# A time-mix layer with a routed feed-forward: VectorE results left in PSUM, right-hand sides with time on the partitions, solves in 32x64 tiles

## The chip, the core and the metric

One core of one Trainium2 chip. The time is device time of one launch, in microseconds (us). TensorE, VectorE, ScalarE and GpSimd are called PE, DVE, ACT and POOL in the profile; SP is the queue that issues most DMAs.

## What is computed

The input is x, 8 sequences of 512 steps with 256 channels (16 heads of 16). Cut to what matters:

```python
r, k, v, w, kk, a = projections(x, previous x)      # kk normed per head, b = -kk * a
wt = exp(-exp(w))
def step(s, inp):                                   # s: 16 x 16 for each sequence and head
    q_, w_, k_, v_, a_, b_ = inp
    sa = einsum('bhij,bhj->bhi', s, a_)
    s = s * w_[:, :, None, :] + sa[..., None] * b_[:, :, None, :] + v_[..., None] * k_[:, :, None, :]
    return s, einsum('bhij,bhj->bhi', s, q_)
y = group_norm(scan(step)) * ln_w + ln_b + bonus    # bonus = (r * k * faaaa).sum(head) * v
x1 = layer_norm(x + (y * g) @ Wo.T)
out = layer_norm(x1 + expert(argmax(x1 @ centroids.T), x1))   # 8 experts, 256 -> 1024 -> 256
```

## The kernel before, in words

The 512 steps are cut in 16 blocks of 32 steps (TB); each block is worked on for all 8 sequences and 16 heads at once. Within a block the recurrence is turned into matrix algebra: scores between all pairs of steps (`scores`, L639), the inverse of a unit triangular 32x32 matrix for each of the 128 pairs of sequence and head (GpSimd, `invert`, L1881), and then with R, the right-hand sides, the product of inverse and R (`solve`, L691), read-out (`read_out`, L721), and the next state (`update`, L707, and `next_state`, L1501). All arithmetic is fp32. After the 16 blocks comes a routing stage and then 39 blocks of 128 tokens through the experts, which the change touches only in where two small PSUM results lie.

Each engine runs a fixed list of calls written out by hand, `body(n)` for n from -2 to 18 (TensorE L779, ScalarE L1208, VectorE L1612, SP L508). Body n holds different stages of several blocks: projections and scores of block n+1, transposes of keys and values of block n, the chain R, solve, read-out and state of block n-1, gate and output projection of block n-2, router of block n-3. Nothing is reordered at run time: an engine that waits holds up all that is behind it in its list. Six PSUM banks are a ring, whose order of users is the list at L364; a user of a bank waits until the steps named in `freed` (L351) have read the one before it. The other two banks (`ry_bank`, RY) hold R and the output Y.

What the change touches, in the order of one body on TensorE:

- `read_state` (L665), called for one half f of the channels at the end of a body and for the other half at the start of the next one. Its first loop has 32 matmuls of a 32x32 state tile with a moving operand of 64 columns, 32 that give R and 32 that give the state's part of Y. Its second loop adds the values' part of R, 32 matmuls of 64x32. R comes out with channels on the partitions and time on the columns.
- `keep_r` (VectorE, L1486) copies R with a mask for odd and even heads into Rm, `turn_r` (TensorE, L687) transposes Rm in 2 times 4 transposes of 128x128, and `keep_rt` (ScalarE, L1144) copies the result to RT, with time on the partitions.
- `solve` (L691): for each half, 32 matmuls of 64x64 tiles. The stationary tile holds the inverses of two heads as a block-diagonal matrix whose zeros are written once. Two tiles of the array are used in turn, chosen by e.
- `keep_x` (ScalarE, L1150) and `keep_x_odd` (VectorE, L1495) copy the result into XV.
- The keys' transposes `turn_keys` for the second half stand after `square(n+1, "r")` and after the second `solve`.

A matmul in fp32 is two records of a weight load and two of a matmul in the trace (two passes), so 32 matmuls are "x64" in a PE row.

The inversion runs on GpSimd for block after block: each block is 30 pairs of a multiply (L1894) and an add (L1897). Around it are DMAs, all issued by SP: `scores_to_pairs` (L455) writes the scores to DRAM with 4 DMAs and reads them with one of 512 KB into Up, one (sequence, head) on each partition; `inverse_to_heads` (L470) writes the inverse with one DMA and reads it with 4.

Many VectorE instructions take a projection from a PSUM bank, write an SBUF tile, and a second VectorE instruction then reads two SBUF tiles. Those that matter here: L1378 (four each block), L1410 (k2), L1452 (bt), L1460 (bm, two), L1467 (ao), L1507 (state), L1514 (w). Others read two SBUF tiles before and after the change: L1359, L1366, L1398, L1415 (k3), L1431 (km, two).

## Time and profile before

| | us |
|---|---|
| three runs | 1090.39, 1099.09, 1100.8 (median 1099.09) |
| profiled execution, span from first to last instruction | 1093.4 |
| TensorE busy in it | 1017.8 (93%) |
| VectorE busy | 792.4 (72%) |
| GpSimd busy | 683.2 (62%) |
| ScalarE busy | 542.2 (50%) |
| mean granted TensorE clock | 0.971 |

Of the profiled execution's own time the profile gives the span alone; it lies between the lowest and the median run, 5.7 us under the median. Busy shares are averages over the stages. The blocks take the stretch from about 70 to 745 us, the experts that from 770 us to the end, where GpSimd is nearly idle. Times in a row are us from the start of the span unless they are marked ns; "x64" counts records; a bracket tells how long the engine was idle before and what ended it.

### The profile page before, as it was taken

The numbers are of one execution on the slowest core, as the hardware profiler recorded it, in microseconds if no ns is written. First come the engines' busy times: TensorE is split into PE (matmuls) and PEld (weight loads), VectorE is DVE, ScalarE is ACT, GpSimd is POOL, SyncE is SP. The second block draws the span as 40 slices with busy tenths as digits, with TensorE's granted clock in tenths as the row PEclk, the third lists the DMA queues.
The fourth block names the chain that finished last, engine by engine and source line by source line (L and its number), as shares of the span: only waits on it lengthen the run. The fifth ranks groups of instructions, "written<-read, shape, count | busy, mean of one in ns | idle before, by whom it ended". The sixth has DMA issues, their size and how long they took to land.

```text
span 1093.4 us, 42536 instructions
## 1 busy us (share of the span) xinstructions
PE 1017.8 (93%) x16804; PEld 836.3 (76%) x16805; DVE 792.4 (72%) x1777; ACT 542.2 (50%) x1113; POOL 683.2 (62%) x1135
## 2 busy tenths in 40 slices
PE   8998999999999999999999999589899999999995
PEld 5676777787777786777777778567798988889894
DVE  4776887887887887888888777147466666666663
ACT  4474676686685785776766757122122222222220
POOL 1088888888988988988988869840223332323321
PEclk9998999999999999999999999689999999999998
DMA  4213224134134133243242241828454454545430
GB/s 104 43 18 79 68 35 109 45 68 108 25 89 106 27 89 87 36 98 82 41 98 61 51 99 23 251 62 288 178 184 155 172 167 164 183 145 181 147 127 4
DMA packets 208624, 112.02 MB, mean 102 GB/s; under 512 B 172364, under 2 KB 191952, under 8 KB 208080
## 3 DMA queue, kind: packets, MB, share of 16 engines
q1 hardware_dynamic: 202080, 100.77, 34.1%
q0 software_dynamic: 3744, 8.40, 2.3%
q8 instruction: 122, 2.00, 0.8%
q10 hardware_dynamic: 2640, 0.54, 0.2%
q14 instruction: 38, 0.31, 0.1%
HBM read 85.42 MB, written 26.08 MB: 102 GB/s over the span
## 4 chain that ended last, share of the span: by engine, by line
PE 68%; POOL 13%; DMA 6%; DVE 5%; issue 4%; ACT 1%; SPq 1%; DVEq 0%; ACTq 0%; POOLq 0%
PE bank L561 16%; PE bank L950 12%; PE bank L963 9%; POOL arena L1897 7%; POOL arena L1894 6%; PE bank L699 5%; PE bank L646 5%; PE bank L654 4%; PE ry L963 4%; PE bank L607 3%; PE ry L676 2%; PE ry L728 2%; DMA arena<-scr_n 2%; PE bank L716 1%; DMA arena<-scr_u 1%
## 5 line engine op out<-in xcount | busy, mean ns | idle before, releaser
L1897 POOL TENSOR_TENSOR arena<-arena 128x30 f32<-128x30 f32 (+14 forms) x480 | 295.6, 616 | 37.6
L1894 POOL TENSOR_TENSOR arena<-arena 128x30 f32<-128x30 f32 (+14 forms) x480 | 287.0, 598 | 36.4
L561 PE MATMUL bank<-arena 128*128 128x256 f32 (+2 forms) x992 | 268.3, 408 | 5.6 <-DVE arena L1400 2.7
L561 PEld LDWEIGHTS bank<-arena 128*128 128x128 f32 x992 | 173.3, 196 | 51.7 <-issue 25.4
L950 PEld LDWEIGHTS bank<-arena 128*128 128x128 f32 x1248 | 146.9, 194 | 5.5 <-issue 2.7
L950 PE MATMUL bank<-arena 128*128 128x128 f32 x1248 | 147.4, 277 | 3.2 <-DVE arena L1803 2.5
L1482 DVE TENSOR_TENSOR arena<-bank,arena 128x512 f32<-128x512 f32 x128 | 79.5, 683 | 29.6 <-PE bank L646 29.5
L1293 ACT ACTIVATE arena<-arena 128x1 f32<-128x1 f32 x39 | 11.5, 294 | 176.9 <-DVE arena L1757 176.9
L1928 POOL COPY arena<-arena 128x1 int32 (+1 forms) x39 | 7.1, 181 | 146.7 <-DVE arena L1821 146.7
L963 PE MATMUL bank<-arena 128*128 x416 | 96.4, 385 | 0.1
L699 PEld LDWEIGHTS bank<-arena 64*64 64x64 f32 x2048 | 68.3, 145 | 28.2 <-issue 22.5
L699 PE MATMUL bank<-arena 64*64 64x32 f32 x2048 | 71.4, 228 | 18.1 <-DMA arena<-scr_u 18.1
L963 PEld LDWEIGHTS bank<-arena 128*128 128x128 f32 x416 | 76.9, 190 | 14.4 <-issue 4.9
L654 PE MATMUL bank<-arena 128*128 128x128 f32 x560 | 80.2, 279 | 1.8 <-issue 0.8
L1922 POOL DMA_INDIRECT arena<-scr_x,arena x39 | 41.1, 1053 | 61.2 <-POOL arena L1920 30.3
L654 PEld LDWEIGHTS bank<-arena 128*128 128x128 f32 x560 | 64.0, 142 | 19.6 <-issue 13.4
L646 PE MATMUL bank<-arena 32*128 32x64 f32 x2048 | 68.8, 275 | 9.4 <-issue 8.2
L646 PEld LDWEIGHTS bank<-arena 32*128 32x128 f32 x2048 | 63.8, 188 | 13.5 <-issue 11.1
L1375 DVE SCALAR_TENSOR_TENSOR arena<-bank,arena 128x256 f32<-128x256 f32 x128 | 55.7, 476 | 19.0 <-PE bank L579 19.0
L1930 POOL DMA_INDIRECT out_dram<-arena x39 | 39.7, 1018 | 34.9 <-DVE arena L1787 20.8
L1803 DVE TENSOR_SCALAR arena<-bank,arena 128x128 f32<-128x128 f32 x156 | 44.0, 345 | 23.1 <-issue 18.0
L1308 ACT ACTIVATE arena<-bank,arena 128x128 f32<-128x128 f32 x156 | 44.7, 368 | 26.6 <-PE bank L950 26.5
(174 smaller groups left out, 1775.2 us busy)
## 6 DMA issues: line engine op xcount, KB each, us to landing
arena<-in_W SPq DMA_DIRECT2D x47, 1024.0 KB, 5.0
scr_n<-arena SPq DMA_DIRECT2D x64, 128.0 KB, 2.8
arena<-scr_n SPq DMA_DIRECT2D x16, 512.0 KB, 3.7
scr_u<-arena SPq DMA_DIRECT2D x16, 512.0 KB, 2.8
arena<-scr_u SPq DMA_DIRECT2D x62, 128.0 KB, 2.9
arena<-in_xTp SPq DMA_DIRECT2D x32, 132.0 KB, 4.0
arena<-in_x SPq DMA_DIRECT2D x64, 64.0 KB, 2.1
scr_x<-arena SPq DMA_DIRECT2D x64, 64.0 KB, 2.5
```

Of the source, the lines that this page charges most:

```text
L561: mm = pe.matmul(ring.tile(m, name)[0:rows, to], lhsT, rhs, start=(i == 0), stop=(i == len(terms) - 1))
L646: mm = pe.matmul(ring.tile(m, f"sc{f}{p}")[:, b * 2 * TB:(b + 1) * 2 * TB], bkm[r, f * B + b, :], aq[m % 2][r, f * B + b].rearrange("p x t ...
L654: mm = pe.transpose(ring.tile(m, name)[:, i * P:(i + 1) * P], src, ident)
L699: mm = pe.matmul(ring.tile(m, f"x{f}")[x, at:at + 32], Ux[m % 2][x, f, p, k].rearrange("p h t -> p (h t)"), RT[f][x, k, 32 * p:32 * p + 32 ...
L950: mm = pe.matmul(hidT_ps[t // 4][:, (t % 4) * P:(t % 4 + 1) * P], W1[s][:, k, t * P:(t + 1) * P], xnT[:, k, :], start=(k == 0), stop=(k == ...
L963: mm = pe.matmul(y_ps[s][:, 0:D], hidT[s][:, t, :], W2f[:, bass.ds(e * (FT * D) + t * D, D)], start=(t == 0), stop=(t == FT - 1))
L1308: relu_act.inc(str(t), A(hidT[s][:, t], hidT_ps[0][:, t * P:(t + 1) * P], ACT.Relu, bias=b1f[:, bass.ds(e * FT + t, 1)]))
L1375: xm_ok.inc(m, f"{g}{h}", STT(out=xm[g][:, h], in0=ring.tile(m, f"lo2_{g}")[:, h * COLS:(h + 1) * COLS], scalar=prm(f"maa{g}", h), in1=dx[ ...
L1482: score.inc(m, name, TT(sc[m % 2][:, f, p].rearrange("p k e x t -> p (k e) (x t)"), ring.tile(m, name)[:, :].rearrange("p (b n) -> p b n", ...
L1803: relu_dve.inc(str(t), nc.vector.tensor_scalar(hidT[s][:, t], hidT_ps[1][:, (t - 4) * P:(t - 3) * P], b1f[:, bass.ds(e * FT + t, 1)], 0.0, ...
L1894: inv_ok.inc(f"m{s}", TT(t, U[:, 0:s, s:s + 1].broadcast_to(shape), U[:, s:s + 1, s + 1:TB].broadcast_to(shape), ALU.mult))
L1897: inv_ok.inc(f"a{s}", TT(U[:, 0:s, s + 1:TB], U[:, 0:s, s + 1:TB], t, ALU.add))
```

## The change

Four edits.

1. VectorE leaves intermediate results in the PSUM bank that they came from: `xm_stage` (L1370), `key_gain` and `gain_keys`, `normed_kk`, `removal`, `decay_kk`, `mask_removal`, `next_state`, `normed`. The second instruction of each pair has then one input in PSUM and one in SBUF. The banks come free later (`freed`), "ao" and "bt" change places.
2. R comes out of `read_state` with time on the partitions: stationary and moving operand are exchanged for R, so the first loop has 64 matmuls with 32 columns each in place of 32 with 64. `keep_r` moves to ScalarE as two plain copies; `turn_r` and `keep_rt` are gone.
3. `solve` works on pairs of head pairs, 32 matmuls each of 32x64 tiles, in four positions of the array in turn, two row groups by two column halves, each row group with a PSUM bank of its own. A product has both heads' inverse times both heads' columns; the half that is not wanted is masked in the copies, `keep_x` (VectorE, six instructions of 64x256 each block) and `keep_x_even` (ScalarE, four of 64x128). The inverse's tile has no zeros and half the size. The scores' read becomes 8 DMAs of 64 KB in place of one of 512 KB.
4. Both `turn_keys` of the second half stand earlier in TensorE's list, their copies on ScalarE too; the first of them now waits in the ring for k2 (bank 5, after "ma").

```diff
-        Ux = [v.rearrange("p (f g k h t) -> p f g k h t", f=HALF, g=PAIRS, k=4, h=2)
-              for v in (Ux_flat[:, 0:2048], Ux_flat[:, 2048:4096])]
+        Ux = [v.rearrange("p (f k e h t) -> p f k e h t", f=HALF, k=4, e=2, h=2)
+              for v in (Ux_flat[:, 0:1024], Ux_flat[:, 1024:2048])]
...
-        Rm_flat = take(NB // 2 * P)
-        Rm = Rm_flat.rearrange("p (g o h t) -> p g o h t", g=NB // 2, o=2, h=2)
-        RT = [take(4 * P).rearrange("p (k n) -> p k n", k=4) for _ in range(HALF)]
+        Rs = take(NB * TB).rearrange("p (e g i) -> p e g i", e=2, g=NB // 2)
...
         ring = Ring(banks, [(0, "bk00@5"), (1, "h@2 k@3"), (0, "bk01@2"), (1, "z@1 a@4 kk@5"), (-3, "logit@2"),
-                            (-2, "g@0"), (1, "ma@5 mk@2"), (-1, "rt0@3 rt1@4"), (-2, "wo@0"), (-1, "x1@1"),
-                            (1, "ss@0 r@4"), (0, "bk11@5"), (1, "v@2"), (-1, "x0@3"), (0, "bk10@0 v0@1 v1@4"),
+                            (-2, "g@0"), (1, "ma@5 mk@2"), (-2, "wo@0"), (-1, "x0@1 x1@3"),
+                            (0, "bk11@5"), (1, "ss@0 r@4"), (0, "bk10@5"), (1, "v@2"), (-1, "x2@1 x3@3"), (0, "v0@5 v1@4"),
...
+        heads_of = lambda m, p: Ux[m % 2][pair_rows(p)].rearrange("r f k e h t -> r (f k e h) t")
...
-                sp.dma_start(Up[m % 2].rearrange("p r c -> p (r c)"),
-                             nd.rearrange("f g k e (h s) t -> (f g k e h) (s t)", h=2)).then_inc(n_in, 16)
+                for f in range(HALF):
+                    for p in range(PAIRS):
+                        sp.dma_start(Up[m % 2][32 * p + 16 * f:32 * p + 16 * f + 16].rearrange("p r c -> p (r c)"),
+                                     nd[f, p].rearrange("k e (h s) t -> (k e h) (s t)", h=2)).then_inc(n_in, 16)
...
+                for p in range(PAIRS if m < last else 2):
+                    sp.dma_start(heads_of(m, p), u_rows[p]).then_inc(u_in, 16)
...
                 for b in range(B):
                     for p in range(PAIRS):
                         r = slice(32 * p, 32 * p + 32)
-                        pe.matmul(RY[b % 2][r, f * 4 + b // 2], S[r, f * B + b, :], aq[buf][r, f * B + b],
+                        pe.matmul(RY[b % 2][r, f * 4 + b // 2, 0], aq[buf][r, f * B + b, 0], S[r, f * B + b, :],
                                   start=(f == 0 and b // 2 == 0), stop=False, skip_group_check=True)
+                        pe.matmul(RY[b % 2][r, f * 4 + b // 2, 1], S[r, f * B + b, :], aq[buf][r, f * B + b, 1],
+                                  start=False, stop=False, skip_group_check=True)
                 for b in range(B):
                     for p in range(PAIRS):
                         r = slice(32 * p, 32 * p + 32)
                         v = v_rows_of(b % 2)
-                        mm = pe.matmul(RY[b % 2][r, f * 4 + b // 2, 0], XV[buf][v, f * B + b, r],
-                                       sc[buf][v, f, p, b // 2, b % 2, 0], start=False, stop=False, skip_group_check=True)
+                        mm = pe.matmul(RY[b % 2][r, f * 4 + b // 2, 0], sc[buf][v, f, p, b // 2, b % 2, 0],
+                                       XV[buf][v, f * B + b, r], start=False, stop=False, skip_group_check=True)
                 if f == HALF - 1:
                     chain_pe.inc(m, "R", mm)
 
-            def turn_r(m, f):
-                chain_dve.wait(pe, m, "rme", "rmo")
-                turn(m, f"rt{f}", [Rm_flat[:, (f * 4 + k) * P:(f * 4 + k + 1) * P] for k in range(4)])
-
-            def solve(m, f):
-                ring.wait_empty(pe, m, f"x{f}")
-                chain_act.wait(pe, m, f"rt{f}")
+            def solve(m, w):
+
+                pairs = (2 * w, 2 * w + 1)
+                for p in pairs:
+                    ring.wait_empty(pe, m, f"x{p}")
+                chain_act.wait(pe, m, "re", "ro")
                 pe.wait_ge(u_in, (m + 1) * 64)
-                for k in range(B // 2):
-                    for p in range(PAIRS):
-                        for e in range(2):
-                            x, at = x_rows_of(e), k * P + 32 * p
-                            mm = pe.matmul(ring.tile(m, f"x{f}")[x, at:at + 32], Ux[m % 2][x, f, p, k].rearrange("p h t -> p (h t)"),
-                                           RT[f][x, k, 32 * p:32 * p + 32], start=True, stop=True)
-                ring.fill(m, f"x{f}", mm)
-
-            def x_kept(m, f):
-                chain_act.wait(pe, m, f"x{f}e")
-                chain_dve.wait(pe, m, f"x{f}o")
+                mm = {}
+                for g in range(NB // 2):
+                    for turn in range(2):
+                        for i, p in enumerate(pairs):
+                            e, r = (turn + i) % 2, pair_rows(p)
+                            mm[p] = pe.matmul(ring.tile(m, f"x{p}")[x_rows_of(e), g * 32:(g + 1) * 32],
+                                              Ux[m % 2][r, g // 4, g % 4, e].rearrange("p h t -> p (h t)"), Rs[r, e, g, :],
+                                              start=True, stop=True)
+                for p in pairs:
+                    ring.fill(m, f"x{p}", mm[p])
+
+            def x_kept(m):
+                chain_act.wait(pe, m, "x2a", "x2b", "x3a", "x3b")
+                chain_dve.wait(pe, m, "x0e", "x0o", "x1e", "x1o", "x2o", "x3o")
...
                     keep_busy(2, idle_ps)
                 if has(n - 1):
-                    solve(n - 1, 1)
+                    solve(n - 1, 0)
+                if has(n) and n < last:
+                    turn_keys(n, 1, 1)
                 if has(n + 1):
                     norms(n + 1)
                 if -1 <= n <= 0:
                 if has(n + 1):
                     square(n + 1, "r", 0, 0)
                 if has(n) and n < last:
-                    turn_keys(n, 1, 1)
+                    turn_keys(n, 1, 0)
                 if has(n + 1):
                     square(n + 1, "v", 2, 3)
                 if n == -1:
                     keep_busy(3, ry_bank[0])
                 if has(n - 1):
-                    solve(n - 1, 0)
-                if has(n) and n < last:
-                    turn_keys(n, 1, 0)
+                    solve(n - 1, 1)
                 if has(n):
                     turn_values(n, 0)
...
+            def keep_r(m):
+                if m:
+                    ring.wait_full(act, m - 1, "x2", "x3")
+                chain_pe.wait(act, m, "R")
+                for e, name in enumerate("eo"):
+                    chain_act.inc(m, f"r{name}", A(Rs[:, e], RY[e][:, :, 0], ACT.Copy))
+
+            def keep_x_even(m, p):
+                ring.wait_full(act, m, f"x{p}")
+                x = x_rows_of(0)
+                for h, name in enumerate("ab"):
+                    i = slice(HS * h, HS * h + HS)
+                    chain_act.inc(m, f"x{p}{name}", A(XV[m % 2][x, 0:NB:2, pair_rows(p)][:, :, i],
+                                                      ring.tile(m, f"x{p}")[x, 0:256].rearrange("p (g i) -> p g i", i=32)[:, :, i],
+                                                      ACT.Copy, scale=own_head[x, h:h + 1]))
...
-                    xm_ok.inc(m, f"{g}{h}", STT(out=xm[g][:, h], in0=ring.tile(m, f"lo2_{g}")[:, h * COLS:(h + 1) * COLS],
-                                                scalar=prm(f"maa{g}", h), in1=dx[:, h], op0=ALU.add, op1=ALU.mult))
+                    part = bank[:, h * COLS:(h + 1) * COLS]
+                    xm_ok.inc(m, f"{g}{h}", STT(out=part, in0=part, scalar=prm(f"maa{g}", h), in1=dx[:, h],
+                                                op0=ALU.add, op1=ALU.mult))
                 xm_ok.wait(dve, m, f"{g}1")
-                xm_ok.inc(m, f"x{g}", TT(tt(xm[g]), tt(xm[g]), x_now, ALU.add))
+                xm_ok.inc(m, f"x{g}", TT(tt(xm[g]), by_step(bank), x_now, ALU.add))
...
-                comb.inc(m, "k2", TT(flat(kt), flat(kt), flat(ma), ALU.mult))
+                comb.inc(m, "k2", TT(flat(kt), flat(kt), ring.tile(m, "ma")[:, :], ALU.mult))
...
-                comb.inc(m, "kkn", STT(out=flat(kk), in0=ring.tile(m, "ss")[:, :], scalar=1e12, in1=flat(kk), op0=ALU.min, op1=ALU.mult))
+                comb.inc(m, "kkn", STT(out=ring.tile(m, "ss")[:, :], in0=ring.tile(m, "ss")[:, :], scalar=1e12, in1=flat(kk), op0=ALU.min, op1=ALU.mult))
...
+                comb.wait(dve, m, "kkn", "ao")
+                bank = ring.tile(m, "ss")[:, :]
+                comb.inc(m, "bt", STT(out=bank, in0=bank, scalar=-1.0, in1=flat(at), op0=ALU.mult, op1=ALU.mult))
...
                 proj.wait(dve, m, "iW0", "iW1")
                 comb.wait(dve, m, "bt")
+                removed = by_step(ring.tile(m, "ss")).rearrange("p (k e) t -> p k e t", e=2)
                 for h in range(2):
-                    comb.inc(m, f"bm{h}", TT(bkm_q[:, :, 1:3, h], pair(at), pair(iW[h]), ALU.mult))
+                    comb.inc(m, f"bm{h}", TT(bkm_q[:, :, 1:3, h], removed, pair(iW[h]), ALU.mult))
...
-                comb.inc(m, "ao", TT(aq[m % 2][:, :, 0], tt(kk), Wt[:, :, 0:TB], ALU.mult))
+                comb.inc(m, "ao", TT(aq[m % 2][:, :, 0], by_step(ring.tile(m, "ss")), Wt[:, :, 0:TB], ALU.mult))
...
+            def keep_x(m, p, e):
+                ring.wait_full(dve, m, f"x{p}")
+                x = x_rows_of(e)
+                chain_dve.inc(m, f"x{p}{'eo'[e]}", TT(XV[m % 2][x, e:NB:2, pair_rows(p)],
+                                                      ring.tile(m, f"x{p}")[x, 0:256].rearrange("p (g i) -> p g i", i=32),
+                                                      same_head[x, None, :].broadcast_to([P // 2, NB // 2, 32]), ALU.mult))
...
                 chain_pe.wait(dve, m, "R")
                 ring.wait_full(dve, m, "su")
-                state_dve.inc(m, "sa", TT(S, ring.tile(m, "su")[:, :].rearrange("p (g i) -> p g i", g=NB), S, ALU.add))
+                su = by_step(ring.tile(m, "su"))
+                state_dve.inc(m, "sa", TT(su, su, S, ALU.add))
                 state_dve.wait(dve, m, "sa")
                 comb.wait(dve, m, "wend")
-                state_dve.inc(m, "s", TT(S, S, Wend[m % 3][:, :, None].broadcast_to([P, NB, 32]), ALU.mult))
+                state_dve.inc(m, "s", TT(S, su, Wend[m % 3][:, :, None].broadcast_to([P, NB, 32]), ALU.mult))
...
                 post_act.wait(dve, m, "rstd", "c0", "c1")
-                post_dve.inc(m, "n", TT(flat(yc), flat(yc), ring.tile(m, "var")[:, :], ALU.mult))
+                bank = ring.tile(m, "var")[:, :]
+                post_dve.inc(m, "n", TT(bank, flat(yc), bank, ALU.mult))
                 post_dve.wait(dve, m, "n")
                 comb.wait(dve, m, "u")
-                post_dve.inc(m, "w", TT(flat(yc), flat(yc), flat(ut[m % 3]), ALU.add))
...
                 if has(n - 2):
                     token_stats(n - 2)
                 if has(n - 1):
-                    keep_x_odd(n - 1, 1)
+                    for p in (0, 1):
+                        keep_x(n - 1, p, 0)
+                        keep_x(n - 1, p, 1)
                 if has(n + 1):
                     key_exponent(n + 1)
                     normed_kk(n + 1)
                     decay_reads(n + 1)
+                    decay_kk(n + 1)
                     removal(n + 1)
-                    decay_kk(n + 1)
                     decay_keys(n + 1)
                     bonus_terms(n + 1)
                 if has(n - 1):
-                    keep_x_odd(n - 1, 0)
+                    keep_x(n - 1, 2, 1)
+                    keep_x(n - 1, 3, 1)
                 if has(n + 1):
```

## Rows read from the trace of the kernel before

**Rows 1.** The page: engines, instruction queue, and DMA issues (size, us to landing).
```profile
PE 1017.8 (93%) x16804; PEld 836.3 (76%) x16805; DVE 792.4 (72%) x1777; ACT 542.2 (50%) x1113; POOL 683.2 (62%) x1135
...
q8 instruction: 122, 2.00, 0.8%
...
arena<-scr_n SPq DMA_DIRECT2D x16, 512.0 KB, 3.7
```

**Rows 2.** Waits of PE from 90 to 700 us: total, times, longest.
```profile
PE bank L699 <- DMA arena<-scr_u: 16.2, 6, 9.7
PE bank L646 <- issue: 8.2, 9, 1.6
```

**Rows 3.** Timeline of PE: the first solve of blocks 0 and 13.
```profile
99.97 2.29 PE L699 MATMUL bank<-arena 64*64 64x32 f32 x51 [2.50 <-DMA arena<-scr_u]
...
656.25 1.96 PE L699 MATMUL bank<-arena 64*64 64x32 f32 x61 [1.17 <-DMA arena<-scr_u]
```

**Rows 4.** Busy by stretch, GpSimd alone: one inversion in mid-run, and the last.
```profile
431.75:473.66 41.91, 37.28 (x61) 1.00 0.34 76
687.97:723.45 35.48, 30.86 (x61) 0.71 0.60 175
```

**Rows 5.** Timelines of POOL and of DVE at 406 us.
```profile
406.64 2.99 POOL L1894 TENSOR_TENSOR arena<-arena 128x240 f32<-128x240 f32 x1
409.70 0.66 POOL L1897 TENSOR_TENSOR arena<-arena 128x240 f32<-128x240 f32 x1
...
406.66 1.27 DVE L1460 TENSOR_TENSOR arena<-arena 128x512 f32<-128x512 f32 x2
407.86 1.28 DVE L1431 TENSOR_TENSOR arena<-arena 128x512 f32<-128x512 f32 x2
```

**Rows 6.** Timeline of PE in one body.
```profile
509.68 1.10 PE L676 MATMUL ry<-arena 32*32 32x64 f32 x64
510.70 0.76 PE L682 MATMUL ry<-arena 64*32 64x32 f32 x64
511.39 0.66 PE L654 MATMUL bank<-arena 128*128 128x128 f32 x4
...
517.99 1.92 PE L561 MATMUL bank<-arena 128*128 128x8 f32 x12
...
520.90 1.09 PE L654 MATMUL bank<-arena 128*128 128x128 f32 x8
521.83 1.89 PE L561 MATMUL bank<-arena 128*128 128x256 f32 x8
523.66 2.06 PE L699 MATMUL bank<-arena 64*64 64x32 f32 x64
...
534.03 0.76 PE L728 MATMUL ry<-arena 128*32 128x32 f32 x64
```

**Rows 7.** Timeline of DVE in the same body.
```profile
519.95 0.87 DVE L1520 SCALAR_TENSOR_TENSOR arena<-arena,bank 128x256 f32<-128x256 f32 x2 [1.66 <-PE bank L561]
...
523.83 0.69 DVE L1530 TENSOR_TENSOR arena<-bank,arena 128x512 f32<-128x512 f32 x1 [0.49 <-PE bank L561]
...
525.99 0.65 DVE L1498 COPY arena<-bank 64x512 f32<-64x512 f32 x1
...
529.95 1.17 DVE L1467 TENSOR_TENSOR arena<-arena 128x512 f32<-128x512 f32 x1
531.05 1.11 DVE L1415 TENSOR_TENSOR arena<-arena 128x512 f32<-128x512 f32 x1
...
532.87 0.67 DVE L1498 COPY arena<-bank 64x512 f32<-64x512 f32 x1
```

**Rows 8.** Busy by stretch: us, busy (records) of PE, PEld, DVE, ACT, POOL, clock.
```profile
447.19:470.49 23.30, 21.61 (x760) 17.21 (x761) 20.45 (x35) 15.55 (x27) 21.09 (x29) 1.00 0.22 50
495.39:510.83 15.44, 14.23 (x501) 11.13 (x506) 12.05 (x21) 8.12 (x16) 13.72 (x23) 1.00 0.28 58
```

**Rows 9.** SP's issues of the scores' writes: count, ns min/median/max of one.
```profile
L462 SPq DMA_DIRECT2D scr_n<-arena x64: 574/648/1695, 40.7 to 679.8; - x64
```

**Rows 10.** Timeline of PE: both solves of the last block.
```profile
730.84 5.92 PE L699 MATMUL bank<-arena 64*64 64x32 f32 x128 [1.94 <-DMA arena<-scr_u]
736.69 2.05 PE L728 MATMUL ry<-arena 128*32 128x32 f32 x128
```

124 lines of the change are left out of this document (51 added, 73 removed).

## Prediction

> **What bounds the kernel now.** I read the page first: TensorE is busy 93% of the span, GpSimd 62% [rows 1], and GpSimd is nearly idle behind the blocks, so within them both are close to full. The share alone doesn't say which one ends last. The timeline of PE says how long a body is: the first solve of block 0 starts at 99.97 us, that of block 13 at 656.25, 13 bodies of 42.8 us [rows 3]. An inversion on GpSimd takes 41.9 us from its first instruction to the last [rows 4], so GpSimd works through block after block with about a microsecond to spare, and TensorE is as full. The waits of PE settle who holds whom: six times PE waited at the solve for the inverse's DMA, 16.2 us in total, of which 9.7 are one wait near the end [rows 2]; the rest, 6.5 us, is 0.5 us a body. The other large group is "issue", time in which PE had no instruction although nothing held it. So PE's own list is the longer loop by a hair, GpSimd's loop touches it, and from block 14 on, where PE has less to do, GpSimd ends last.
>
> Two details decide this case. First, what a crowd of small matmuls costs. In two stretches made mostly of them, PE and PEld together have 1521 records in 23.30 us and 1007 in 15.44 us [rows 8]: 15.3 ns a record in both, whatever the mix. "Issue" waits fall in just these stretches, and the instruction queue moved 2.00 MB in 122 pieces, 16 KB each [rows 1]. 2.00 MB by PE's and PEld's 33,609 records is 60 B a record, so a piece holds some 256 of them (an estimate), and 256 records at 15.3 ns are 3.9 us. I read this as a supply limit: a long crowded stretch can't run faster than a piece each 3.9 us. Second, VectorE. From the fill of the gate's bank (517.99 + 1.92 = 519.91) to the first read-out (534.03) PE takes 14.1 us [rows 6]. VectorE's list in the same stretch starts at 519.95 and ends with a copy at 532.87 + 0.67 = 533.54, with a gap of 0.49 in it [rows 7]. Read-out needs that copy. VectorE is 0.5 us from being the bound of this stretch.
>
> **The change part by part.**
>
> *PSUM results.* A GpSimd instruction of 0.66 us took 2.99 at 406.64, while VectorE ran two bm and two km instructions, all with two SBUF inputs [rows 5]. The last inversion, with VectorE mostly idle, takes 35.48 us, one in mid-run 41.91 [rows 4]: VectorE costs GpSimd 6.4 us a block. By my count 18 VectorE instructions a block read two SBUF tiles and 11 of them stop doing so: 6.4 x 11/18 = 3.9 us; bounds 0 and 6.4. The inversion falls to 38.0 us. What this is worth is only what PE waited for it: -0.5 us a body. VectorE itself gains at ao (1.17 us to the 0.69 that instructions with a PSUM input take) and perhaps at k3 (1.11), which keeps two SBUF inputs [rows 7].
>
> *Transposes of R.* Gone: 8 transposes, 1.09 us busy and 0.93 to the next start (520.90 to 521.83) [rows 6], on PE's list: -0.9. ScalarE's two plain copies stand in a part of its list with slack.
>
> *Solves.* Before, two 64x64 tiles in turn: 64 records in 2.06 us [rows 6]. Now four tile positions in turn. The nearest rows with more positions are the read-outs' and R's 64 records at 0.66 to 0.76 us; with no gain it stays 2.06. I take 1.1 each, so -1.9 a body; bounds -2.7 and 0.
>
> *But these two stand in the stretch in which VectorE is close.* PE's 14.1 us would fall to 11.3. VectorE's 13.1 us of work (13.6 less the gap) lose 0.5 at ao and 0 to 0.4 at k3, and get six masked copies for two: the nearest instruction, two of 128x256 in 0.87 us [rows 7], gives 0.43 each, 2.6 for the 1.3 of before: +1.3. So 13.1 - 0.5 + 1.3 = 13.9, or 13.5 with k3. PE waits there for VectorE, and of the 2.8 us it saves 0.2 to 0.6 is left. I take -0.5. Whether the new tiles overlap hardly matters. The new wait of the keys' transposes for k2 is hidden in this too: k2 ends two VectorE instructions, 1.3 us, behind the output projection, and the solve before it takes 1.1.
>
> *read_state.* It gains 64 matmuls a body: 128 pairs of load and matmul, 256 records, less 16 records for the transposes. It lies right in the crowded stretch, after scores and update. Below: the rate of R's two loops together, 128 pairs from 509.68 to 511.39, 1.71 us, or 13.4 ns a pair [rows 6]: 128 pairs, +1.7 us. At the least it could be nothing, since columns times matmuls stay the same. Above: the rate of rows 8, 256 x 15.3 = 3.9 us. Old stretches were not at the limit all the time, new ones will be nearer to it; I take +2.5. Nothing hides it: the wait for VectorE is in the other half of the body.
>
> The Trainium skill ("Runtime: NRT & Kernel Launch", Instruction fetch mechanics) says that crossing a 16 KiB boundary is "mostly hidden", because dispatch is slower than the fetch. By it nothing is added to the issue cost and the sum would stand at the lower 1.7, some 10 us less over the run; the issue waits in small matmuls speak against it here.
>
> *DMAs.* One read of 512 KB (3.7 us to landing [rows 1]) becomes eight. SP spends 0.65 us on an issue of this kind [rows 9], so the last starts 4.5 us later and lands sooner after its issue: together about +1.8 us, between 0 and +4. GpSimd has 4 us of slack by then, so it costs nothing in mid-run, but counts once before the first inversion and once before the last.
>
> *Sum.* Body: -0.5 - 0.5 + 2.5 = +1.5 us, to 44.3. 13 bodies: +19.5. Start: PE's first wait of 2.50 [rows 3] shrinks with the faster inversion: -2. From the scores of block 14 to those of 15: +1.5. The last DMA: +1.8, the last inversion -0.5. The last solves, 5.92 us [rows 10], run on four tiles: -2.4; but read-out must now wait for all copies instead of the first solve's: +1. Total +18.9 us. The profiled execution's span of 1093.4 becomes 1112.3; the runs' median is 5.7 above the span, which I carry over: 1099.1 + 18.9 = 1118.
>
> **Rivals.** *The extra matmuls are free* (18%). Four tiles stream at once and 64 columns become two times 32, so read_state stays at 1.71 us; the supply limit is my reading of an average. Then a body is -0.5 - 0.5 = -1.0, 13 bodies -13, start, tail and the body between -3: 1083, faster. It decides where read_state adds less than 1 us a body. For it: the columns streamed are the same. Against: rows 8, and 128 records of 64 and 32 columns already run at one rate.
>
> *Only the issue cost, and VectorE frees itself* (20%). +1.7 for read_state, k3 and the masked copies at their best (-0.6): body +0.6, 13 bodies +8, edges +1: 1108, no change that a measurement tells.
>
> *The full supply price* (12%): +3.9, or pairs on the same tile that don't overlap, which come to about the same. Body +2.9, 13 bodies +38, edges as in the forecast: 1137.
>
> *The PSUM edit does not do what it says*: inversions stay at 41.9. With bodies of 44.3 GpSimd still isn't the bound, and the time stays within 2 us of the forecast; it is inside it. The trace would show it.
>
> **How the numbers follow.** Forecast 50%, with a range of its own from 1108 to 1130. About 1% (11 us) is what a measurement of this kernel tells from no change. Faster by more: the first rival, 0.18. Within 1% (1088 to 1110): the second rival and the low end of the forecast, 0.28. Slower: 0.54. The range 1085 to 1138 takes in the second and most of the third rival and leaves about 2 in 10 outside, mostly the first. The edits to GpSimd, transposes and solves all point to less time; that the sum comes out above zero rests on one term, read_state.
>
> The Trainium skill ("TensorEngine Tiling (Array Packing)", Instruction Overhead) states about 60 cycles a matmul, the same for 1 column as for 60. By that, as an estimate, the split doubles the first loop, 1.02 us to 2.04 in each call, +2.0 a body in place of +2.5 and about 1111 in all; no row here shows a 32x32 tile with 32 columns.
>
> **What would show it.** Inversions of about 38 us. No wait of PE for the inverse before block 14. Body of about 44.3 us. L676's successors with 128 records each plus 64 of the second loop in 2.7 us or more. Rather more "issue" in the crowded stretch; rows of 256 records at 3.9 us there. PE waiting for VectorE before the first read-out or in the solves' stretch, 1 to 2 us a body. Wrong: read_state at 1.7 to 2.0 us with bodies under 42.3, or PE without any wait between gate and read-out.

## The result, and the profile after

The changed kernel takes 1175.4 us against 1099.9 for the kernel before: ratio 1.068, with an interval of 1.063 to 1.074. I had said 1118, with a range up to 1138. The sign was right, the size a quarter of what came. In the profiled executions the span grew by 82.1 us, from 1093.4 to 1175.5.

First the page of after, to compare with [rows 1]:

```profile
PE 1029.9 (88%) x18724; PEld 825.1 (70%) x18725; DVE 771.7 (66%) x1809; ACT 534.8 (45%) x1145; POOL 623.2 (53%) x1135
...
q8 instruction: 137, 2.24, 0.8%
...
arena<-scr_n SPq DMA_DIRECT2D x128, 64.0 KB, 2.6
```

The granted clock in fortieths of the span (tenths of 2.4 GHz, 9 is 90% or more), the page of before:

```profile
PEclk9998999999999999999999999689999999999998
```

and of after:

```profile
PEclk9998898999988999989889998857999999999998
```

TensorE's busy time grew by 12 us, the span by 82: the time is idle time and slower time, not work. The mean granted clock is 0.935 where it was 0.971. With levels of 1.2 and 2.4 GHz that is 2 x 0.065 x 1175.5 = 153 us at the low level against 2 x 0.029 x 1093.4 = 63.

The length of a body comes from the first solves of blocks 0 and 13, as in [rows 3] (timeline of PE):

```profile
102.45 1.82 PE L705 MATMUL bank<-arena 32*64 32x32 f32 x60 [1.44 <-ACT arena L1051]
...
722.26 1.85 PE L705 MATMUL bank<-arena 32*64 32x32 f32 x64 [2.50 <-DMA arena<-scr_u]
```

(722.26 - 102.45) / 13 = 47.7 us, where it was 42.8. 13 bodies make 63.5 of the 82 us; 2.5 come before them and 16.1 after.

The waits of PE from 90 to 700 us, against [rows 2] (total, times, longest):

```profile
PE ry L688 <- issue: 23.3, 11, 2.5
PE bank L705 <- DMA arena<-scr_u: 7.8, 4, 2.4
PE ry L736 <- issue: 7.3, 7, 1.4
PE bank L650 <- issue: 6.7, 11, 1.2
PE bank L658 <- DVE arena L1424: 5.5, 8, 0.7
PE ry L680 <- issue: 5.1, 6, 1.5
PE bank L658 <- DVE arena L1434: 4.5, 12, 0.4
```

and the only large wait of GpSimd in the same stretch; in before it was 12.5 us in 6 waits:

```profile
POOL arena L1898 <- DMA arena<-scr_n: 120.5, 13, 14.5
```

The largest group is "issue" in the second loop of `read_state`, L688: nothing that the profile shows holds TensorE there, and it has no instruction. An inversion, busy by stretch as in [rows 4], now takes 37.7 us, and GpSimd then stands still until the next scores are in, 8.0 us here and 9.3 on average (120.5 / 13):

```profile
376.29:413.96 37.67, 33.04 (x61) 0.95 0.32 62
```

One stall in full (timeline of PE, one call of `read_state`, the first and last groups of its first loop, then the second loop):

```profile
463.43 0.27 PE L680 MATMUL ry<-arena 32*32 32x32 f32 x7
...
464.66 0.22 PE L682 MATMUL ry<-arena 32*32 32x32 f32 x3
464.82 0.64 PE L688 MATMUL ry<-arena 64*32 64x32 f32 x50
467.64 0.29 PE L688 MATMUL ry<-arena 64*32 64x32 f32 x14 [2.18 <-issue]
```

The first loop, now 64 matmuls and so 128 records, takes 464.82 - 463.43 = 1.39 us; with 32 matmuls of 64 columns, 64 records, it took 1.02 [rows 6]. Where instructions are at hand, 64 records more cost 0.37 us. Then, 50 records later, none are left for 2.18 us.

The trace also tells what these stalls are. PE's and PEld's records grew by 3,840 and the instruction queue by 15 pieces: 256 records a piece, as the prediction had estimated. Counted in PE's whole list, 39 of the 40 issue waits of over 0.3 us between 90 and 700 us (53.4 of 54.3 us; in before 23 of 24, 20.2 us) end at the same place of a piece: the number of records before them leaves 193 to 195 when divided by 256. Two examples, busy by stretch, each from inside one of these stalls to inside the next (PE and PEld stand first; with PE's five other instructions each stretch holds 512, two pieces):

```profile
457.50:466.50 9.00, 6.87 (x254) 4.71 (x253) 5.18 (x10) 3.14 (x5) 1.41 (x5) 0.81 0.43 100
505.90:513.80 7.90, 5.60 (x254) 4.18 (x253) 5.38 (x12) 4.11 (x5) 0.00 (x0) 1.00 0.29 53
```

By the DMA records of the instruction queue, the transfer of a piece ended at 466.22 and PE went on at 467.64. So it is at 34 of the 35 issue waits of over 0.7 us: PE goes on 1.2 to 1.6 us behind the end of a piece's transfer. The first loop uses up 256 records (128 of matmuls and 128 of loads) in 1.39 us; from 500.06 to 515.85 five pieces started 3.8 to 4.1 us apart, and nowhere from 90 to 700 us were two closer than 3.4. The stalls are waits for instructions to be fetched.

Last, a view that I hadn't taken for the prediction: SP's own timeline. First the kernel before, from the scores' writes of a block to the inverse's reads:

```profile
338.91 1.29 SPq L462 DMA_DIRECT2D scr_n<-arena  x2
342.17 0.34 SPq L467 DMA_DIRECT2D arena<-scr_n  x1
342.56 2.28 SPq L452 DMA_DIRECT2D scr_x<-arena  x4
344.94 1.80 SPq L444 DMA_DIRECT2D arena<-in_x  x4
346.83 0.37 SPq L475 DMA_DIRECT2D scr_u<-arena  x1
349.64 2.53 SPq L486 DMA_DIRECT2D arena<-scr_u  x4
```

Then after:

```profile
357.58 7.17 SPq L467 DMA_DIRECT2D scr_n<-arena  x4
367.99 6.39 SPq L474 DMA_DIRECT2D arena<-scr_n  x8
374.42 1.85 SPq L457 DMA_DIRECT2D scr_x<-arena  x4
376.37 1.81 SPq L449 DMA_DIRECT2D arena<-in_x  x4
378.29 0.37 SPq L482 DMA_DIRECT2D scr_u<-arena  x1
381.04 2.57 SPq L491 DMA_DIRECT2D arena<-scr_u  x4
```

The solves that these reads serve (timeline of PE), in before:

```profile
355.68 2.06 PE L699 MATMUL bank<-arena 64*64 64x32 f32 x64
```

and in after:

```profile
386.14 1.13 PE L705 MATMUL bank<-arena 32*64 32x32 f32 x64 [1.55 <-DMA arena<-scr_u]
```

The write of a block's inverse (scr_u) stands in SP's list behind the read of the next block's scores (scr_n). Before, GpSimd finished the inversion at 345.7 and its write was issued at 346.8. After, GpSimd had finished at 361.8 and the write went out at 378.3. This is one of the longest such waits: 6.2 us of its 16.5 pass before the reads begin, 6.4 in the issues of the eight reads, 3.9 in what follows them. In most bodies of after from 180 us on, the reads begin within about 3 us of the inversion's end and the write follows their first issue by 9.3 to 10.6 us, where in before, from 300 us on, it was 4.7 to 6.6. The eight reads hold up not only the next inversion but the finished one.

### The profile page after: what moved, and what is told of

Its sections match the earlier page's. It is cut to its first block, busy times and chain, and to the rows that moved or that the text cites. A ratio compares the mean times of both kernels' runs of the same rounds, so it can differ in the third digit from the quotient of the medians.

```text
span 1175.5 us, 46538 instructions
## 1 busy us (share of the span) xinstructions
PE 1029.9 (88%) x18724; PEld 825.1 (70%) x18725; DVE 771.7 (66%) x1809; ACT 534.8 (45%) x1145; POOL 623.2 (53%) x1135
## 4 chain that ended last, share of the span: by engine, by line
PE 62%; DVE 13%; issue 9%; DMA 8%; SPq 3%; ACT 3%; POOL 1%; DVEq 0%; ACTq 0%; POOLq 0%
PE bank L565 13%; PE bank L957 11%; PE bank L970 8%; PE bank L650 6%; PE ry L970 4%; PE bank L658 3%; SPq L474 2%; PE bank L611 2%; DMA arena<-scr_u 2%; DMA scr_n<-arena 2%; PE ry L680 2%; PE bank L705 2%; PE ry L736 2%; DVE arena L1505 2%; PE bank L724 2%
## 5 line engine op out<-in xcount | busy, mean ns | idle before, releaser
L565 PE MATMUL bank<-arena 128*128 128x256 f32 (+2 forms) x992 | 284.0, 425 | 10.5 <-DVE arena L1414 5.0
L1908 POOL TENSOR_TENSOR arena<-arena 128x30 f32<-128x30 f32 (+14 forms) x480 | 268.6, 560 | 37.6
L1905 POOL TENSOR_TENSOR arena<-arena 128x30 f32<-128x30 f32 (+14 forms) x480 | 253.6, 528 | 36.4
L565 PEld LDWEIGHTS bank<-arena 128*128 128x128 f32 x992 | 179.8, 204 | 68.9 <-issue 36.6
L957 PE MATMUL bank<-arena 128*128 128x128 f32 x1248 | 147.5, 277 | 3.1 <-DVE arena L1814 2.5
L1898 POOL MEMSET arena<- 128x32 f32 x16 | 2.5, 156 | 194.1 <-DMA arena<-scr_n 194.1
L1498 DVE TENSOR_TENSOR arena<-bank,arena 128x512 f32<-128x512 f32 x128 | 79.6, 684 | 34.6 <-PE bank L650 34.6
L658 PE MATMUL bank<-arena 128*128 128x128 f32 x432 | 75.7, 303 | 14.4 <-DVE arena L1424 6.8
L1389 DVE SCALAR_TENSOR_TENSOR bank<-bank,arena 128x256 f32<-128x256 f32 x128 | 56.1, 484 | 46.5 <-PE bank L583 46.5
L658 PEld LDWEIGHTS bank<-arena 128*128 128x128 f32 x432 | 55.2, 155 | 36.4 <-issue 23.1
L650 PEld LDWEIGHTS bank<-arena 32*128 32x128 f32 x2048 | 65.2, 191 | 14.9 <-issue 12.3
L1420 DVE TENSOR_TENSOR arena<-bank,arena 128x512 f32<-128x512 f32 x16 | 11.1, 692 | 84.7 <-PE bank L611 84.7
L705 PE MATMUL bank<-arena 32*64 32x32 f32 x2048 | 39.9, 229 | 24.4 <-DMA arena<-scr_u 19.1
L705 PEld LDWEIGHTS bank<-arena 32*64 32x64 f32 x2048 | 36.5, 144 | 34.8 <-issue 16.0
L680 PEld LDWEIGHTS ry<-arena 32*32 32x32 f32 x2048 | 43.9, 107 | 23.1 <-issue 22.9
```

Of the source, the lines that this page charges most:

```text
L565: mm = pe.matmul(ring.tile(m, name)[0:rows, to], lhsT, rhs, start=(i == 0), stop=(i == len(terms) - 1))
L650: mm = pe.matmul(ring.tile(m, f"sc{f}{p}")[:, b * 2 * TB:(b + 1) * 2 * TB], bkm[r, f * B + b, :], aq[m % 2][r, f * B + b].rearrange("p x t ...
L658: mm = pe.transpose(ring.tile(m, name)[:, i * P:(i + 1) * P], src, ident)
L680: pe.matmul(RY[b % 2][r, f * 4 + b // 2, 0], aq[buf][r, f * B + b, 0], S[r, f * B + b, :], start=(f == 0 and b // 2 == 0), stop=False, ski ...
L705: mm[p] = pe.matmul(ring.tile(m, f"x{p}")[x_rows_of(e), g * 32:(g + 1) * 32], Ux[m % 2][r, g // 4, g % 4, e].rearrange("p h t -> p (h t)") ...
L957: mm = pe.matmul(hidT_ps[t // 4][:, (t % 4) * P:(t % 4 + 1) * P], W1[s][:, k, t * P:(t + 1) * P], xnT[:, k, :], start=(k == 0), stop=(k == ...
```

## The experiments

Two theories stood at first. A: the 64 added matmuls a body stand in a crowd of small ones, in which instructions come in too slowly. B: the other layout, banks held longer and waits for VectorE cost it. Bodies are measured as above, from block 0 to block 13.

**psum_only**: the kernel before with VectorE's results left in PSUM, and

```diff
-(0, "bk10@0 v0@1 v1@4")
+(0, "bk10@5 v0@1 v1@4")
```

> The kernel before with the first part of the change alone: VectorE's intermediate results stay in PSUM, the banks come free later, the last keys' transpose goes to another bank. Theory A (the loss is in the supply of TensorE's instructions, this part is harmless): inversions of 37 to 38 us, no wait of TensorE for the inverse in mid-run, body 42 to 42.5 us, ratio to before 0.985 to 0.995. Rival B (banks held longer make TensorE wait, part of the 75 us is lost here): ratio over 1.01, with waits of TensorE for VectorE of over 1 us a body.

Measured: 0.992 (0.988 to 0.995). Inversions fell to 36.7 us, even more than I had forecast, the body stayed at 42.8, and no wait for VectorE of any size came in. This part does what it says, and by the medians is worth 9 us. Where they come from isn't shown: the profiled execution was the slowest of its seven, 1092.3 us from first to last instruction against 1093.4 in before. B falls for this part.

**split_r**: the kernel before with the same 64 matmuls more, and nothing else.

```diff
-pe.matmul(RY[b % 2][r, f * 4 + b // 2], S[r, f * B + b, :], aq[buf][r, f * B + b],
+for x in range(2):
+    pe.matmul(RY[b % 2][r, f * 4 + b // 2, x], S[r, f * B + b, :], aq[buf][r, f * B + b, x],
```

> The kernel before, but each of read_state's first-loop matmuls is two of 32 columns in place of one of 64: 64 matmuls a body more, nothing else changed, no other layout, no other wait. Theory A: read_state grows from 3.9 to 6.5 to 7.5 us a body, with issue waits in its second loop, body 45.5 to 46.5 us, ratio 1.035 to 1.05, and the mean clock falls from 0.971 to about 0.95. My forecast's own price (2.5 us a body) would be ratio 1.03. Rival B (the other layout and its waits are what costs): ratio 1.00 to 1.01.

Measured: 1.054 (1.049 to 1.058), body 47.1 us, clock 0.950. Waits of PE, 90 to 700 us (L683 is the second loop, L677 the first):

```profile
PE ry L683 <- issue: 22.9, 11, 3.6
PE ry L677 <- issue: 7.8, 11, 1.6
```

This is after's picture, from this edit alone: 59 us, 3.7 a block, and above the 1.05 that theory A had allowed. Its issue waits end at the same place of a 256-record piece as after's (39 of 40, 49.0 us).

**wide_place**: the same number and shape of small matmuls, but 16 each ahead of the wide matmuls of k, r, v and the gate.

```diff
+for i in range(16):
+    r, at = slice(32 * (i % 4), 32 * (i % 4) + 32), 32 * (i // 4)
+    pe.matmul(ring.tile(m, name)[r, at:at + 32], w_sq[r, 3, 0, 0:32], w_sq[r, 3, 1, 0:32], start=True, stop=True)
```

> The kernel before with 64 more small matmuls a block, 32x32 tiles with 32 columns as those that split_r adds, but ahead of the wide matmuls of k, r, v and the gate, 16 each; their results are overwritten. Theory A (instructions come in at a limited rate, wide matmuls let them catch up): only the issue cost of 0.9 to 1.5 us a body, ratio 1.015 to 1.03, no new issue waits at these places. Rival C (an added small matmul costs some 65 ns wherever it stands, as in split_r): 4 us a body, ratio 1.05.

Measured: 1.023 (1.014 to 1.031), clock 0.967: 25 us, 1.6 a block, give or take 9 us. The same count costs 59 us in the crowd. By the length of a body it is +2.4 us (45.2) against +4.3 (47.1). So the place decides about half of the price. A stands.

**no_y**: after without the state's part of Y. **spread**: after with the second `read_state` behind the projection of k.

```diff
-pe.matmul(RY[b % 2][r, f * 4 + b // 2, 1], S[r, f * B + b, :], aq[buf][r, f * B + b, 1],
```

> The kernel after without the 64 matmuls a body that add the state's part to the output Y (that part of the computation is left out). Theory A: read_state back to about 4 us a body, body 43.5 to 44.5, ratio to the kernel before 1.01 to 1.03 in place of 1.068. Rival B: ratio 1.05 to 1.07.

> The kernel after with the second call of read_state moved behind the keys' first transpose, the hidden layer and the projection of k, so that wide matmuls stand between its two calls; the number of instructions is the same. Theory A (it is the crowd that costs, wide matmuls give the supply time to catch up): 1 to 2 us a body less than after, ratio to before 1.04 to 1.055, issue waits in read_state gone or halved. Rival C (each small matmul costs the same wherever it stands): ratio 1.06 to 1.075.

Measured: no_y 1.040 (1.035 to 1.046), which neither theory had: TensorE now waited for the inverse 15 times from 90 to 740 us, 61.2 us in all. Something else holds the body at 45.4 us once the crowd is smaller. spread 1.087 (1.081 to 1.093): a miss. The issue waits in the second loop fell from 23 to 16 us, but the hidden layer now stood ahead of R and waited for VectorE (L1392, 9.8 us in 12), and the clock fell to 0.927. It moved too much at once to tell on A.

**fillers** and its control **before_fillers**: two useless matmuls of 256 columns between the loops of each `read_state`.

```diff
+ahead, name = (m + 2, "lo2_1") if f == 0 else (m + 1, "bk00")
+if ring.takes(ahead, name):
+    ring.wait_empty(pe, ahead, name)
+    keep_busy(2, ring.tile(ahead, name))
```

> The kernel after with two matmuls of 256 columns (0.43 us each at 2.4 GHz) between the two loops of each read_state, into a bank that is free: 1.7 us a body of work that nobody needs. If the stalls of read_state are a supply limit, the fillers stand in time that is lost anyway, issue in its second loop falls from 25 us to under 10, and the cost is under half of their 1.7 us; if TensorE's idle time there is also what brings the half clock, its time falls from 155 us to under 110 and the ratio to 1.055 or less. If neither holds: ratio 1.085 to 1.095.

> The kernel before with the same two matmuls of 256 columns in each read_state as in fillers. Here the stalls are short (4 us in all), so there is little for the fillers to stand in: 1.2 to 2 us a body, ratio 1.015 to 1.03. That they cost nothing in after (1.0585 against 1.0682) is then the stall and the clock of after. If they cost nothing here either, the fillers say nothing on after's stalls: ratio under 1.01.

Measured: after with fillers 1.059 (1.049 to 1.068), no slower than after (1.063 to 1.074) although more is done; that it is faster isn't shown, since the intervals overlap. Before with them 1.016 (1.012 to 1.020), 17 us slower. In after the issue wait of the second loop fell from 23.3 to 13.3 us, and the mean clock rose from 0.935 to 0.958: 2 x 0.042 x 1163.5 = 98 us at the low level in place of 153. The marks set for A were under 10 us of issue wait, under 110 us at the low level, and 1.055 or less: only the second was reached. That the fillers stand in stall time is shown. That the stalls bring the low clock, which then costs more, fits these numbers; the two were not parted.

**keys_later**: after with both moved transposes, and ScalarE's copies of them, further back.

```diff
-(0, "bk11@5"), (1, "ss@0 r@4"), (0, "bk10@5"), (1, "v@2"),
+(1, "ss@0 r@4"), (0, "bk11@5"), (1, "v@2"), (0, "bk10@5"),
```

> The kernel after with the two moved transposes of the keys further back: one behind the projection of r, one behind that of v, and ScalarE's copies of them moved back too. If the new wait for k2 costs (5.5 us in 8 waits of after, and 4.5 us for k's masked copy), 0.5 to 0.8 us a body comes back: ratio 1.055 to 1.06. If it is hidden in a wait for VectorE that comes anyway, as I forecast, or if the crowd of small matmuls behind it takes it back: 1.065 to 1.07.

Measured: 1.063 (1.055 to 1.072). The waits at L658 for VectorE are gone, and 12.3 us at a projection (L565, for e2) stand in their place. Its interval overlaps after's: no gain is shown.

**no_y_four_reads**: the second bound, first try: the scores' read in 4 DMAs.

```diff
-for f in range(HALF):
-    for p in range(PAIRS):
-        sp.dma_start(Up[m % 2][32 * p + 16 * f:32 * p + 16 * f + 16].rearrange("p r c -> p (r c)"),
-                     nd[f, p].rearrange("k e (h s) t -> (k e h) (s t)", h=2)).then_inc(n_in, 16)
+for p in range(PAIRS):
+    sp.dma_start(Up[m % 2][pair_rows(p)].rearrange("p r c -> p (r c)"),
+                 nd[:, p].rearrange("f k e (h s) t -> f (k e h) (s t)", h=2)).then_inc(n_in, 16)
```

> no_y (the kernel after without the state's part of the output) with the scores' read in 4 DMAs of 128 KB in place of 8 of 64 KB. Theory D (in no_y the bound is the round through SP's list: the inverse's write stands behind the issues of the scores' read, so each of them costs 0.65 us a body): 4 issues less are 2.6 us, TensorE's wait for the inverse falls from 61 us to 20 to 35, ratio from 1.040 to 1.00 to 1.02. Rival: the transfers themselves set the round; ratio 1.035 to 1.045.

Measured: 1.111 (1.102 to 1.121), far slower, body 51.5 us. SP's timeline:

```profile
340.02 2.60 SPq L473 DMA_DIRECT2D arena<-scr_n  x4
...
347.49 0.37 SPq L481 DMA_DIRECT2D scr_u<-arena  x1
356.24 2.23 SPq L490 DMA_DIRECT2D arena<-scr_u  x4
```

and, from the view of the DMAs, GB/s in fortieths of the 12 us from 341 to 353:

```profile
GB/s 0 14 0 0 27 55 55 55 51 246 137 167 188 89 65 65 109 205 79 184 184 150 140 147 321 423 396 423 355 41 55 41 55 55 55 55 55 55 48 34
```

The busy share of the 16 DMA engines, in tenths, in the same slices:

```profile
DMA  0200011119456221372665549999811111111110
```

The issues are shorter as planned (2.6 us for the 4.3 to 6.4 of eight), but the reads flow at some 55 GB/s at either end of the stretch, and the inverse's write of 512 KB waits behind them: 8.7 us to landing, where it took 2.7. These DMAs have an outermost dimension of 2. The Trainium skill ("DMA: Bandwidth & Descriptors", Why a DMA increments its semaphore by 16 and not by 1) says that the slowest dimension sets the number of DMA engines used, so 2 here. The trace agrees: in the slices of 55 GB/s the busy share is one tenth, and 2 engines of 16 are 0.125. As a test of the issues' price it failed; it does show that time added on this way is paid in full.

**y_later** and **y_later_mixed**: after with the state's part of Y moved among the next body's projections; in the second also low_2 and a keys' transpose between the loops of `read_state`. Nothing is left out.

```diff
     square(n + 1, "k", 1, 2)
+if has(n - 1):
+    state_to_y(n - 1, 0)
...
     decay_a_kk(n + 1)
+if has(n - 1):
+    state_to_y(n - 1, 1)
```

> The kernel after with the 64 matmuls for the state's part of Y taken out of read_state and put among the projections of the next body: 32 behind k, 32 behind decay, a and kk. All work is done, the instruction count is the same. Theory A (the crowd costs, by the supply and the clock; among wide matmuls 64 of them cost 1.6 us a body as in wide_place, in the crowd 4.3 as in split_r): 2 to 3 us a body less than after, half-clock time well under 155 us, ratio 1.03 to 1.045. If the cost were in the layout or in waits for VectorE: ratio 1.06 or more. As the round of the inverse was the bound of no_y at a body of 45.7 us, it may stop the gain at 1.04.

> y_later with the rest of read_state's crowd broken up too: low_2 (block n+2) between the two loops of the first call, the keys' first transpose between those of the second. Theory A: issue waits in read_state under 8 us in all. The time is then set by the round of the inverse through SP's queue, at a body of 45 us or more: waits of TensorE for the inverse of 20 us or more in all, ratio 1.025 to 1.045. Without that round as a bound it would be 1.01 to 1.025.

Measured: 1.059 (1.055 to 1.062) and 1.060 (1.056 to 1.064). The issue waits in `read_state` are mostly gone, the time hardly moved, and TensorE waits for the inverse: 27.1 us in 10 bodies, and 43.4 in 14 (90 to 740 us). The faster its own list, the longer it waits: bodies are 46.6 and 47.2 us.

**before_8reads**: the kernel before with only the read split.

```diff
-sp.dma_start(Up[m % 2].rearrange("p r c -> p (r c)"),
-             nd.rearrange("f g k e (h s) t -> (f g k e h) (s t)", h=2)).then_inc(n_in, 16)
+for f in range(HALF):
+    for p in range(PAIRS):
+        sp.dma_start(Up[m % 2][64 * f + 16 * p:64 * f + 16 * p + 16].rearrange("p r c -> p (r c)"),
+                     nd[f, p].rearrange("k e (h s) t -> (k e h) (s t)", h=2)).then_inc(n_in, 16)
```

> The kernel before, the scores' read as 8 DMAs of 64 KB in place of one of 512 KB, same rows, nothing else. Theory E (the round from a block's solve over the scores, their read, the inverse's write behind it in SP's list and back to the solve is the second bound): in before it takes 24 us from solve to the scores' copies and 17 to the next solve, 41 us, hidden under a body of 42.6; 4.2 us of issues more make 45, so the body becomes 44.5 to 45.5, TensorE waits 1.5 to 3 us a body for the inverse, ratio 1.03 to 1.05. My forecast's view (the later read is hidden in GpSimd's slack, only the first and last inversion count): ratio 1.00 to 1.005.

Measured: 1.067 (1.064 to 1.071), as much as the whole change. TensorE's largest wait from 90 to 700 us:

```profile
PE bank L701 <- DMA arena<-scr_u: 38.5, 13, 4.3
```

GpSimd's:

```profile
POOL arena L1889 <- DMA arena<-scr_n: 99.1, 13, 10.0
```

and SP's timeline:

```profile
378.36 4.28 SPq L469 DMA_DIRECT2D arena<-scr_n  x8
382.68 1.86 SPq L452 DMA_DIRECT2D scr_x<-arena  x4
384.64 3.06 SPq L444 DMA_DIRECT2D arena<-in_x  x4
387.80 0.37 SPq L477 DMA_DIRECT2D scr_u<-arena  x1
390.53 2.14 SPq L488 DMA_DIRECT2D arena<-scr_u  x4
```

Every body waits 3 us for the inverse, and the clock is 0.935, as in after. The body is 48.7 us, and the ratio is above the 1.03 to 1.05 that theory E gave. The issues explain 4 of the 5.9 us. The low clock can explain the rest: from 90 to 700 us it holds for 102 us where it was 41, so 8.2 us a body for 2.9, which at half speed costs at most 2.7 us a body (an estimate). It comes behind the waits. Each of the 11 waits for the inverse of 1.9 us or more from 140 us on is followed by a stretch at the low level, as here (by stretch; the wait from 392.3 to 395.2, then what follows; the third number from the end is the clock):

```profile
392.30:395.20 2.90, 0.00 (x0) 0.01 (x1) 2.20 (x7) 2.78 (x5) 2.62 (x4) 1.00 1.03 159
395.80:402.60 6.80, 6.80 (x59) 5.25 (x56) 2.66 (x4) 1.78 (x3) 6.09 (x10) 0.50 0.15 24
```

**after_sp, y_later_sp, y_later_mixed_sp, psum_sp, all_moved**: x1's stores and the token loads no longer stand between the scores' read and the inverse's write.

```diff
-if has(n - 2) and n - 2 < last - 1:
-    load_tokens(n - 2)
 if has(n - 1):
     inverse_to_heads(n - 1)
+if n <= last and has(n - 3):
+    store_x1(n - 3)
...
+if n <= last and has(n - 1):
+    load_tokens(n - 1)
 if has(n + 1):
     scores_to_pairs(n + 1)
```

> The kernel after with SP's list in another order: the stores of x1 and the loads of tokens no longer stand between the scores' read and the inverse's write. Theory E: the round is 4 to 5 us shorter, but the crowded instructions hold the body near 47 us, so only the 10 us of waits for the inverse and something of the jitter come back: ratio 1.055 to 1.065. If the round were what sets the time of after: 1.04 or less.

> y_later (1.0585) with SP's list in the same other order. Theory E: waits for the inverse fall from 27 us to under 8, body from 46.6 to 44 to 45, ratio 1.02 to 1.04. Rival (PE's own list, the wait for ScalarE's copy of R and the clock hold it): ratio 1.05 or more.

> y_later_mixed (1.060) with SP's list in the same other order. Its own work without the waits for the inverse was 44.2 us a body (47.3 less 3.1): ratio 1.015 to 1.035, and below y_later_sp by up to 0.01 if the crowd counts once the round is out of the way.

Measured: after_sp 1.060 (1.056 to 1.064), y_later_sp 1.026 (1.022 to 1.031), y_later_mixed_sp 1.026 (1.021 to 1.031); bodies of 47.0, 44.9 and 44.6 us. Taking out one bound of after gives 1.0 (y_later) or 0.8 (after_sp) points, each give or take 0.7, taking out both 4.2. Two bounds side by side look like this.

> The kernel before with VectorE's results in PSUM (psum_only: 0.9917) and SP's list in the other order. The round of the inverse is then 36 to 37 us under a body of 42.3, so it holds nothing back: only the jitter of single bodies and some of 4 us of waits for the inverse can go; ratio 0.985 to 0.992. If GpSimd or the round touched the body more often than the waits show: 0.98 or less.

> y_later_mixed_sp (1.0259) with the two keys' transposes further back as in keys_later. If the new waits of TensorE for VectorE there (k2 and k's masked copy, about 10 us in all) are what is left: ratio 1.015 to 1.02. If a wait for VectorE only moves to the next instruction, as keys_later on after suggested (no more than 0.005 gained): 1.022 to 1.028.

Measured: psum_sp 0.994 (0.991 to 0.997), all_moved 1.031 (1.025 to 1.037), above both of its ranges: no gain. **psum_mixed**, psum_only with `read_state`'s loops parted by low_2 and a transpose:

> The kernel before with VectorE's results in PSUM (psum_only, 0.9917) and read_state's two loops parted in the same way: low_2 between them in the first call, the keys' first transpose in the second. No work is added. If the crowd costs in the kernel before as well (4.9 us issue in the second loop, 72 us at half clock), ratio 0.98 to 0.99. If the supply is only late elsewhere then: 0.99 to 0.995.

gave 0.994 (0.991 to 0.997). Neither psum_sp nor psum_mixed adds to psum_only: the kernel before has neither bound above its body. No version is shown to beat the first part alone, 0.992.

## Why the prediction was right and wrong

- PSUM results: right. 38.0 us forecast for an inversion, 37.7 in after; the body didn't gain, since GpSimd had not set it.
- Solves and transposes: right. 1.1 us for each solve, 1.13 measured (386.14); before it was 2.06 [rows 6].
- What that leaves at VectorE: half right. I had PE waiting for VectorE 1 to 2 us a body; the rows of after have 5.5 + 4.5 us and a few more in 13 bodies, about 1 us a body, though at the keys' transposes and not before read-out. "No wait of PE for the inverse before block 14" was wrong: 7.8 us in 4 waits. "The new wait for k2 is hidden" was wrong in place, but all_moved and keys_later say that it costs nothing by itself.
- read_state, "+2.5 with bounds of 1.7 and 3.9": the mechanism, a supply limit, was right, the size short. Split_r, the same 64 matmuls, costs 59 us, 3.7 a block. The step that failed is the one that marked the added records down from the supply price, because "old stretches were not at the limit all the time". In a crowd the 256 added records (240 net in after) are about one more piece a body, 3.9 us by the prediction's own upper bound, and the pieces did come 3.8 to 4.1 us apart. The lower bound was misread too: "128 records of 64 and 32 columns already run at one rate" is not what [rows 6] show. There 64 records of 64 columns take 1.02 us and 64 of 32 columns 0.69; by the second rate the new first loop takes 1.38 us, and 1.39 was measured. So the issue of the added records costs 0.37 us a call; the price is in stalls like the 2.18 us one, and in what I had no term for at all, the clock: 153 us at the low level for 63.
- The reads, the step that failed worst. "GpSimd has 4 us of slack by then, so it costs nothing in mid-run" priced the later read by its own reader alone. I had counted the issues about rightly (4.5 us for seven more, from [rows 9]; the eight take 4.2 to 6.7), but not named what stands behind them in SP's list: the write of the inverse that GpSimd has just finished. From that write to the solve there was under 1 us of slack: issued at 346.83, reads issued until 352.2, 2.9 us to landing, solve at 355.68. before_8reads shows this edit alone at 6.7%.
- The edges: "start -2" came out at +2.5 (102.45 for 99.97), since the first inversion waits for the eight reads too. What follows block 13's solve I had at +1.4 and it is +16.1, almost all of it before the first matmul of the routing stage: 117.0 us from block 13's solve to there (839.27) for 101.2 (757.42). The mean clock in this stretch is 0.75 where it was 0.86, 30 us more at the low level, which at half speed explains at most 15 us (an estimate). What brings the clock down there wasn't tried.
- The rivals: the first (extra matmuls free) and the second (only the issue cost) fall by split_r. The third, "full supply price", came nearest, with a body at 45.7. That two bounds each reach a body of 47 to 49 us, so that each alone costs nearly what both cost, was in none.
- The Trainium skill ("Runtime: NRT & Kernel Launch", Instruction fetch mechanics), cited in the prediction for a hidden fetch, doesn't hold here: the same 64 matmuls cost 59 us in the crowd and 25 among wide ones, with issue waits of 31 us in the two loops, and PE goes on only 1.2 to 1.6 us behind the end of a piece's transfer. From the Trainium skill ("TensorEngine Tiling (Array Packing)", Instruction Overhead) I had +1.02 us for a first loop; with instructions at hand it was +0.37.

Open stays what makes up the 2.6% of y_later_sp. The 64 added matmuls at wide_place's price are 2.3 points of it; where the 2 us a body that solves and transposes save then went wasn't settled. Part three without part two wasn't tried, since the solves need R in the new layout. Nor was before_8reads with SP's other order, which would show how much of its 6.7% the reads cost when nothing but them stands before the inverse's write.

## What to carry to other kernels

When an edit turns one DMA into several, look in the issuing engine's own timeline for what is next in its list and who waits for that; the reader's slack is not the measure. When two rounds of the same length run side by side, price each edit on both: the time goes by the longer, and undoing one alone shows almost nothing. Small matmuls were cheap to issue here and dear in a crowd: count the records of a crowd in pieces of 256, price each piece at the time between two of them (3.8 to 4.1 us here), and put small matmuls among wide ones.

## What the runs showed that I had not expected

- Eight issues of 64 KB in place of one of 512 KB, in a kernel otherwise unchanged, cost 6.7%, as much as the whole change.
- The stalls in small matmuls come once in 256 records of PE's list or in a multiple of it, 39 of 40 of them, and the long ones end 1.2 to 1.6 us behind the transfer of a piece.
- Two useless matmuls in each `read_state` cost nothing in the changed kernel (1.059 for 1.068, intervals overlap) and 17 us in the old one.
- Four DMAs of 128 KB with an outermost dimension of 2 were much slower than eight of 64 KB (1.111 against 1.040).
- Waits of TensorE are followed by a lower clock, so that a wait is dearer than its length: in before_8reads the wait of 3 us a body came with a mean clock of 0.935 for 0.971, and bodies grew by 5.9 us.
